# Two quantised feed-forward stages laid out with features on the partitions, two sequences a product, and the second product of a unit four steps behind its first

## The reference, cut to what matters

```python
def _L3_ffn_ref(x, qweights, scales, biases, lora_a, lora_b, ln_gamma, ln_beta):
    def _dequant(q, scale):                       # groups of 16 share a scale
        return (q.astype(jnp.float32) / 7.5 - 1.0) * jnp.repeat(scale, 16, axis=1)
    def _qlora_linear(x, q, scale, bias, la, lb):
        base = jnp.einsum('btd,od->bto', x, _dequant(q, scale)) + bias
        return base + jnp.einsum('btr,or->bto', jnp.einsum('btd,rd->btr', x, la), lb)
    def _layernorm(x, g, b):
        mu = jnp.mean(x, axis=-1, keepdims=True)
        var = jnp.mean(jnp.square(x - mu), axis=-1, keepdims=True)
        return (x - mu) * jax.lax.rsqrt(var + 1e-5) * g + b
    h = x
    for blk in range(3):
        y = _qlora_linear(h, ... 2 * blk ...)
        y = jax.nn.gelu(_layernorm(y, ln_gamma[blk], ln_beta[blk]), approximate=False)
        h = _qlora_linear(y, ... 2 * blk + 1 ...) + h
    return h
...
x = x + 0.5 * _L3_ffn_ref(_layernorm(x), ...)     # stage f3a
x = x + _L3_attn_ref(_layernorm(x), ...)          # stage at3
x = x + 0.5 * _L3_ffn_ref(_layernorm(x), ...)     # stage f3b
```

## Time and profile before

| | us |
|---|---|
| median of 3 runs | 3105.43 (3095.72 to 3110.03) |
| the profiled execution: its own time | 3106.51 |
| its span | 3104.8 |
| stage f3a, first to last instruction | 101.6 |
| stage at3 | 410.0 |
| stage f3b | 100.5 |
| mean granted TensorE clock over the span | 0.896 |

### The profile page before, as it was taken

The page is one execution under the profiler, slowest core; times in us unless marked ns, Lnnn a source line. Parts: engine busy times, 40 slices in busy tenths (PEclk is TensorE's granted clock), DMA queues, the critical chain, the costliest instruction groups (busy, mean ns, idle before and its releaser), DMA issues. The chain is left out here.

```text
span 3104.8 us, 39498 instructions
## 1 busy us (share of the span) xinstructions
PE 2575.9 (83%) x11320; PEld 1549.7 (50%) x11320; DVE 2025.0 (65%) x4275; ACT 1696.5 (55%) x3585; POOL 1243.8 (40%) x1144
## 2 busy tenths in 40 slices
PE   7999785688888888888677998688699967988975
PEld 5667532354444444444333443456444444777764
DVE  7888655699999999999644443466344364545445
ACT  4555322788888888888422443577444323555532
POOL 1000102688888888888500000322000052444444
PEclk9999898798989989989898999799899966888866
DMA  2000131333333434333332111000111100000000
GB/s 99 1 1 0 58 83 28 131 142 136 151 140 139 145 136 150 140 136 148 143 82 82 55 60 50 1 1 0 55 55 55 63 15 0 1 0 0 0 1 14
DMA packets 35669, 209.60 MB, mean 68 GB/s; under 512 B 4032, under 2 KB 5184, under 8 KB 14016
## 3 DMA queue, kind: packets, MB, share of 16 engines
q1 hardware_dynamic: 35520, 207.89, 18.8%
HBM read 205.25 MB, written 2.62 MB: 67 GB/s over the span
## 5 line engine op out<-in xcount | busy, mean ns | idle before, releaser
L1382 PE MATMUL banks<-mam_state_c,identity 128*128 128x512 f32 x1024 | 539.7, 662 | 141.8 <-POOL mam_state_c L1225 141.8
L1225 POOL TENSOR_TENSOR mam_state_c<-mam_state,weights_r 128x1024 f32<-128x1024 f32 x256 | 599.9, 2358 | 118.6 <-DVE mam_state L1173 118.5
L1173 DVE TENSOR_TENSOR_SCAN mam_state<-banks,mam_dbu 128x1024 f32<-128x1024 f32 x256 | 580.4, 2278 | 73.1 <-ACT banks L1301 72.5
L1301 ACT ACTIVATE banks<-mam_dt,mam_a_neg 128x255 f32<-128x255 f32 x1024 | 423.3, 461 | 38.3 <-DVE mam_state L1173 36.7
L1382 PEld LDWEIGHTS banks<-mam_state_c,identity 128*128 128x128 f32 x1024 | 200.1, 208 | 399.1 <-issue 199.6
L1151 DVE TENSOR_TENSOR mam_dbu<-banks,weights_r 128x1024 f32<-128x1024 f32 x224 | 267.1, 1204 | 10.4 <-ACT banks L1309 10.4
L2224 POOL TENSOR_TENSOR at_attention<-at_relu 128x512 f32<-128x512 f32 x128 | 130.9, 1040 | 172.9 <-ACT at_relu L2277 88.3
L424 ACT ACTIVATE at_probs<-banks,at_nmax 128x256 f32<-128x256 f32 x256 | 117.7, 472 | 138.4 <-DVE at_nmax L365 134.9
L2402 PEld LDWEIGHTS banks<-at_v,at_attention 128*128 128x128 f32 x1024 | 153.2, 223 | 41.0 <-issue 34.8
L862 DVE TENSOR_TENSOR m2b_hidden<-m2b_gelu,m2b_comb_spread 128x512 f32<-128x512 f32 x128 | 85.9, 690 | 129.2 <-ACT m2b_gelu L889 119.6
L862 DVE TENSOR_TENSOR m2a_hidden<-m2a_gelu,m2a_comb_spread 128x512 f32<-128x512 f32 x128 | 86.0, 690 | 128.9 <-ACT m2a_gelu L889 118.5
(11 more groups left out here) (483 smaller groups left out, 5304.6 us busy)
## 6 DMA issues: line engine op xcount, KB each, us to landing
weights_r<-mam_bc_rows SPq DMA_DIRECT2D x128, 1024.0 KB, 4.7
m2a_comb_spread<-m2a_comb_rows SPq DMA_DIRECT2D x16, 1024.0 KB, 7.6
m2b_comb_spread<-m2b_comb_rows SPq DMA_DIRECT2D x16, 1024.0 KB, 7.6
m1a_comb_spread<-m1a_comb_rows SPq DMA_DIRECT2D x16, 512.0 KB, 8.1
m1b_comb_spread<-m1b_comb_rows SPq DMA_DIRECT2D x16, 512.0 KB, 8.5
weights_r<-in_mb SPq DMA_DIRECT2D x1, 4332.0 KB, 12.8
weights_r<-in_m SPq DMA_DIRECT2D x1, 4200.0 KB, 13.1
weights_r<-in_a SPq DMA_DIRECT2D x1, 2632.0 KB, 12.1
```

What stands on the lines that cost most here:

```text
L1173: dve.tensor_tensor_scan(flat2(h[:, i % 4, :, :, :]), decay(i), flat2(dbu[:, i % 4, :, :, :]), 0.0, ALU.mult, ALU.add).then_inc(h_ready, 1)
L1225: pool.tensor_tensor(hc[:, j % 4, :, :, :], h[:, j % 4, :, :, :], c_rows(j), ALU.mult).then_inc(hc_ready, 1)
L1301: i = act.activation(decay(j)[:, o + 1:o + S], dt[:, q, c, 1:S], ACT.Exp, scale=aneg[:, l, k:k + 1])
L1382: k = pe.matmul(y_bank(q)[:, :], K.ident[:, :], flat(hc[:, j % 4, n, :, :]), start=(j == 0 and n == 0), stop=(j == NP - 1 and n == 1))
```

## The change

In both stages the activations are kept with features on the partitions, 512 tokens (a pair of sequences) wide. The weights become the stationary operand, so one product handles a pair. A unit is one block for one pair; there are 3 x 4 = 12 of them (n = 4 * block + pair), and the hardware loop is gone. The norm inside a block is rebuilt: the first weights of each block and their bias have their mean over the outputs taken off once, so that y comes out with mean zero; ACT makes y and its square (L2029, L2026), PE sums the squares over the features with four products against one column of ones (L2080), DVE turns the sum into variance plus eps (L1975), POOL takes the power -1/2 of 128x4 numbers (L2002), PE spreads the result over all partitions with four products against the identity (L2071), and DVE multiplies (L1968). The bias of the second product goes into the add of h (L1961). Transposes are left only at the entry and the exit of a stage (L2046, L2103).

The engines walk through steps m = 0 to 16. PE's list in step m holds the second product of unit m-4, the spread of unit m-2, the sum of squares of unit m-1 and the first product of unit m. The first product of unit m >= 4 needs the h that DVE makes out of the second product of unit m-4, the same pair one block earlier.

The weights are built in f3a alone and kept for f3b (K.f3_w, K.f3_b). The stage has 24 semaphores instead of 17. The packed array f3 holds 6 columns of biases instead of 768.

```diff
-    "f3": dict(scale=768, bias=768, la=768, lb=768, gam=3, bet=3),
+    "f3": dict(scale=768, bcol=6, la=768, lb=768, gam=3, bet=3),
...
-    NB, U = 3, 4
+    NB, NP = 3, B // 2
+    N = NB * NP
...
+        w = K.f3_w
+        bcol = K.f3_b
...
+        y_bank = lambda m: K.ps[m % 3]
+        r_bank = lambda m: K.ps[3 + m % 2]
+        z_bank = lambda m: K.ps[5 + m % 2]
+        t_bank = lambda p: (r_bank, z_bank)[p // 2](p)
+        b1 = lambda m: bcol[:, 2 * (m // NP):2 * (m // NP) + 1]
+        b2 = lambda m: bcol[:, 2 * (m // NP) + 1:2 * (m // NP) + 2]
+        v_cols = lambda m: K.ps[7][:, (m % 2) * 8:(m % 2) * 8 + TP]
...
+                norm_sums(0)
+                if first:
+                    dve.wait_ge(K.loaded["f3"], 16)
+                    dve.wait_ge(K.loaded_q, 16)
+                    link = chain(dve, dve_s)
+                    link(dve.tensor_scalar(w[:, :], K.qw[:, :], 7.5, 1.0 / 7.5, ALU.subtract, ALU.mult))
+                    link(dve.tensor_tensor(w[:, :], w[:, :], f("scale"), ALU.mult))
+                norm_apply_pair(0)
+                if first:
+                    dve.wait_ge(lora_ps, 1)
+                    dve.tensor_tensor(w[:, 0:512], w[:, 0:512], K.ps[0][:, :], ALU.add)
+                    link(dve.tensor_tensor(w[:, 512:768], w[:, 512:768], K.ps[1][:, 0:256], ALU.add))
+                    firsts = w[:, :].rearrange("p (b a o) -> p b a o", b=NB, a=2)[:, :, 0, :]
+                    link(dve.tensor_reduce(wmean[:, :], firsts, AX_X, ALU.add))
+                    link(dve.tensor_scalar(wmean[:, :], wmean[:, :], 1.0 / P, None, ALU.mult))
+                    dve.tensor_tensor(firsts, firsts, wmean[:, :].unsqueeze(2).broadcast_to([P, NB, P]), ALU.subtract)
+                    dve.wait_ge(bias_ps, 1)
+                    cols = bcol[:, :].rearrange("p (b a) -> p b a", a=2)
+                    dve.tensor_copy(cols[:, :, 1], f("bcol").rearrange("p (b a) -> p b a", a=2)[:, :, 1])
+                    dve.scalar_tensor_tensor(cols[:, :, 0], K.ps[2][:, 0:6].rearrange("p (b a) -> p b a", a=2)[:, :, 0],
+                                             -1.0 / P, f("bcol").rearrange("p (b a) -> p b a", a=2)[:, :, 0],
+                                             ALU.mult, ALU.add).then_inc(w_ready, 1)
+                    dve.wait_ge(w_ready, 1)
+                norm_sums(1)
+                norm_apply_pair(1)
+                for m in range(N + 5):
+                    n = m - 4
+                    if 0 <= n < N:
+                        dve.wait_ge(z_ps, n + 1)
+                        h = ht[:, n % NP, :]
+                        dve.scalar_tensor_tensor(h, z_bank(n)[:, :], b2(n), h, ALU.add, ALU.add).then_inc(h_ready, 1)
+                    n = m - 2
+                    if 0 <= n < N:
+                        dve.wait_ge(r_ps, n + 1)
+                        dve.wait_ge(y_ready, n + 1)
+                        if n >= 2:
+                            dve.wait_ge(gt_ready, n - 1)
+                        dve.tensor_tensor(yn[:, n % 2, :], yc[:, n % 3, :], r_bank(n)[:, :],
+                                          ALU.mult).then_inc(yn_ready, 1)
+                    n = m - 1
+                    if 0 <= n < N:
+                        dve.wait_ge(var_ps, n + 1)
+                        if n >= 2:
+                            dve.wait_ge(ys_ready, n - 1)
+                        dve.tensor_scalar(var[:, n % 2, :], v_cols(n), 1.0 / P, EPS, ALU.mult,
+                                          ALU.add).then_inc(var_ready, 1)
+                    if m + 2 < NP:
+                        norm_sums(m + 2)
+                        norm_apply_pair(m + 2)
+                    p = m - 5 - (NB - 1) * NP
+                    if 0 <= p < NP:
+                        dve.wait_ge(o_ps, p + 1)
+                        x = K.x[:, p * WP:(p + 1) * WP]
+                        dve.scalar_tensor_tensor(x, y_bank(m)[:, :], 0.5, x, ALU.mult, ALU.add).then_inc(added, 1)
...
+                norm_root(0)
+                norm_root(1)
+                for n in range(N):
+                    if n + 2 < NP:
+                        norm_root(n + 2)
+                    pool.wait_ge(var_ready, n + 1)
+                    if n >= 2:
+                        pool.wait_ge(r_ps, n - 1)
+                    pool.tensor_tensor(ys[:, n % 2, :], var[:, n % 2, :], K.neg_half[:, 0:TP],
+                                       ALU.pow).then_inc(ys_ready, 1)
...
+                transposed_input(0)
+                if first:
+                    act.wait_ge(w_ready, 1)
+                for m in range(N + 2):
+                    n = m - 2
+                    if 0 <= n < N:
+                        act.wait_ge(yn_ready, n + 1)
+                        if n >= 2:
+                            act.wait_ge(z_ps, n - 1)
+                        act.activation(gt[:, n % 2, :], yn[:, n % 2, :], ACT.Gelu, bias=f("bet")[:, n // NP:n // NP + 1],
+                                       scale=f("gam")[:, n // NP:n // NP + 1]).then_inc(gt_ready, 1)
+                    if m < N:
+                        act.wait_ge(y_ps, m + 1)
+                        if m >= 2:
+                            act.wait_ge(var_ps, m - 1)
+                        act.activation(sq[:, m % 2, :], y_bank(m)[:, :], ACT.Square, bias=b1(m)).then_inc(sq_ready, 1)
+                        if m >= 3:
+                            act.wait_ge(yn_ready, m - 2)
+                        act.activation(yc[:, m % 3, :], y_bank(m)[:, :], ACT.Identity, bias=b1(m)).then_inc(y_ready, 1)
+                    if m + 1 < NP:
+                        transposed_input(m + 1)
...
+                transposed_input(0)
+                if first:
+                    pe.wait_ge(w_ready, 1)
+                for m in range(N + 5):
+                    n = m - 4
+                    if 0 <= n < N:
+                        pe.wait_ge(gt_ready, n + 1)
+                        if n < 2:
+                            pe.wait_ge(ht_ready, n + 3)
+                        else:
+                            pe.wait_ge(h_ready, n - 1)
+                        c = 2 * (n // NP) + 1
+                        pe.matmul(z_bank(n)[:, :], w[:, c * P:(c + 1) * P], gt[:, n % 2, :],
+                                  start=True, stop=True).then_inc(z_ps, 1)
+                    n = m - 2
+                    if 0 <= n < N:
+                        pe.wait_ge(ys_ready, n + 1)
+                        if n < 2:
+                            pe.wait_ge(ht_ready, n + 1)
+                        else:
+                            pe.wait_ge(yn_ready, n - 1)
+                        for j in range(TP):
+                            k = pe.matmul(r_bank(n)[:, j * P:(j + 1) * P], ys[:, n % 2, j:j + 1].broadcast_to([P, P]),
+                                          K.ident[:, :], start=True, stop=True)
+                        k.then_inc(r_ps, 1)
+                    n = m - 1
+                    if 0 <= n < N:
+                        pe.wait_ge(sq_ready, n + 1)
+                        if n >= 1:
+                            pe.wait_ge(var_ready, n)
+                        for j in range(TP):
+                            k = pe.matmul(v_cols(n)[:, j:j + 1], sq[:, n % 2, j * P:(j + 1) * P], K.ones[:, 0:1],
+                                          start=True, stop=True)
+                        k.then_inc(var_ps, 1)
+                    if m < N:
+                        p = m % NP
+                        if m >= 3:
+                            pe.wait_ge(y_ready, m - 2)
+                        if m < NP:
+                            pe.wait_ge(ht_ready, m + 1)
+                        else:
+                            pe.wait_ge(h_ready, m - NP + 1)
+                        c = 2 * (m // NP)
+                        pe.matmul(y_bank(m)[:, :], w[:, c * P:(c + 1) * P], ht[:, p, :],
+                                  start=True, stop=True).then_inc(y_ps, 1)
+                        if m + 1 < NP:
+                            transposed_input(m + 1)
+                    p = m - 5 - (NB - 1) * NP
+                    if 0 <= p < NP:
+                        pe.wait_ge(h_ready, (NB - 1) * NP + p + 1)
+                        pe.wait_ge(y_ready, min(N, m - 2))
+                        if p >= 3:
+                            pe.wait_ge(added, p - 2)
+                        for j in range(TP):
+                            k = pe.transpose(y_bank(m)[:, j * P:(j + 1) * P], ht[:, p, j * P:(j + 1) * P], K.ident[:, :])
+                        k.then_inc(o_ps, 1)
...
+        K.f3_w = K.sb("f3_weights", [P, 6 * P])
+        K.f3_b = K.sb("f3_bias", [P, 6])
```

More of the change, by code:

```diff
@@ L1891, in stage_quantised_ffn @@
+        f = lambda n: field(K, "f3", n)
+        first = tag == "f3a"
+        y_bank = lambda m: K.ps[m % 3]
[5 more added lines that the diff above has]
+        v_cols = lambda m: K.ps[7][:, (m % 2) * 8:(m % 2) * 8 + TP]
         with nc.Block() as block:
@@ new lines, in norm_sums, with norm_apply_pair @@
+                def norm_sums(p):
```

(29 more changed lines are left out.)

168 lines of the change are left out of this document (27 added, 141 removed).

## The result

The changed kernel took 3012.66 us (median of 4 runs, 3005.74 to 3027.46) beside 3105.4; the ratio is 0.971 (95% interval 0.967 to 0.976). Five more runs of it had a median of 3019.70 beside 3104.07, ratio 0.973 (0.970 to 0.975). The direction and the source of the gain were as forecast. The profiled execution was the slowest of the four (3027.46 us).

The account below looks back on a forecast made before the run. Bound by a chain crossing the engines phase by phase, with PE's clock low. f3b 63.5 plus f3a 66.2 us instead of 202.1 gives -72.4; semaphores +0.9 and waits +1.5 leave -70: 3035.5 us, range 3021 to 3066.

Parts of the forecast that it names:

- Step: Middle of both stages: PE's four items take 3.47 us unhindered, the root adds 0 to 0.25; 3.60 taken.
- Entry: Stage start: DVE's four norm rounds, then step 3 and half of step 4 at low clock, +4; f3b 24.3 us.
- Weights in f3a: f3a's entry: adds, reduce, subtract and tiny operations make 2.7 us; two earlier operations hide in the first root's wait.
- Exit: End of each stage, after the first product of unit 11: a chain of 10.4 us.
- Unpriced waits, +1.5: Both stages: free banks, first uses, GELU's table load; 0 to 5 us over 17 steps twice, 1.5 taken.
- Semaphores, +0.9: After each stage: seven more semaphores to clear, 0.066 us each, +0.9.
- The other stages: Everything outside f3a and f3b, at3 between them included, was taken as left alone.
- The favourable end: Whole kernel 3025 with step 3.47, clock 1.00 at entry and no waits; below 3025 got 0.03.
- The swing: Middle steps: half run at 6.7 us as PE's clock swings, 25 us in all, 3060; chance 0.18.
- the low level: Both stages at low clock throughout: step 6.7, 25 us more a stage, 3090 in all; chance 0.07.
- The serial chain: In-order lists make units follow one another: step 9.0 us, 3138 in all, slower; chance 0.04.
- That the entry on DVE bounds a part of the stage: Stage entry: DVE binds it, so only the 8 middle steps gain; already in the sum, 24 us of 63.

Follow-up runs that it names:

- the split run: Both large products split into four of 128 columns each, against the changed kernel: f3b 58.70, f3a 62.23 us, step 3.57 us.
- the run with all norms first: Changed kernel with sums earlier, idle products (one in f3a, three in f3b), all four norms and roots ahead of the first unit: f3b 55.30, f3a 60.26 us.
- the run with idle products: Changed kernel with unread identity products ahead of the first transposes, one in f3a, four in f3b: f3b 58.03, f3a 61.56 us.
- half of the second product: Changed kernel with every second product over 256 of 512 columns: step 3.28 us; f3b gained 0.8 us, f3a 2.3.
- the repeat: The changed kernel again, no edit, against the kernel before: ratio 0.973 (0.970 to 0.975), f3a 61.57, f3b 58.03 us.
- the power twice: Changed kernel with POOL taking every unit's power twice: step 4.26 us, f3b 70.28, f3a 72.01, whole 3031.69 us (one run).
- the two runs that leave work out: Changed kernel with half of every second product, or half of every spread, left out: steps of 3.28 and 3.06 us.
- the rebuilt f3b: Changed kernel with f3b building weights, their mean and biases again, as f3a does: f3b 61.58, f3a 63.40 us.
- half of the spread: Changed kernel with two of the four column blocks of every spread left out: step 3.06 us.

## Why the prediction was right in kind and low in size

- **Bound before, source of the gain.** Right. With the units in series nothing of the gain is left, and the split run shows that the width is worth nearly nothing.
- **Step.** 3.47 by the list, 3.60 taken, 3.50 measured; 0.8 us a stage too much. The parts 0.86, 0.94, 0.81, 0.86 came out as 0.86, 0.89, 0.81, 0.94. From the end of the sum to the spread's weight load the root takes 3008.45 to 3009.93, 1.48 us (hop 0.17, power 1.01) against 1.60 to 1.97 forecast: no product waits in front of the spread, but it is the tightest feed, as said. That the power could stretch beside DVE wasn't tested by the step: DVE is idle all through it (1.67 us ahead of 3010.45). "One of DVE's SBUF operations" is too broad as well: in the run with all norms first, a power beside the application of a norm and bn_stats of 128x128 still took 1.03 us.
- **Entry: the step that failed.** "I count these 2.6 us and half of step 4 at the low level, +4". Without it the sum had 20.3 for f3b; 19.86 is measured. PE had not "mostly stood still": from the first product on it was busy nearly throughout, and the level rose 14.9 us after the start, ahead of the spread (17.1 us) from which PE goes on without a wait. The low products are there (2.07 us each), but beside DVE's rounds; the run with idle products removed some of them and gained 0.00, and with the level at 1.00 from 8.8 us on (half of the second product) y3 came no earlier. It was close: PE's sum of unit 1 ends where the third first product starts (2977.14), and DVE, just then ready for it, makes the variance behind that power; a rise 5.5 us later cost 1.83 us in f3a. In f3a the forecast was 27.0 and 23.35 is measured. These two entries are 8.1 of the 10.1 us by which the stages were over-forecast.
- **Weights in f3a.** Forecast 2.7 us, measured 3.5. The adds, the reduce and the small ones took 2.6, as forecast. The two operations that were to hide in the wait for the first root did stand in it, but the root took longer beside them: POOL's scaling and power took 0.44 and 1.72 us instead of 0.23 and 1.03, and DVE's first application came 0.97 us later than in f3b.
- **Exit.** 10.4 forecast; from the end of step 11 (3009.39) to 3019.57, 10.18.
- **Unpriced waits, +1.5.** None seen in the middle; the table load of GELU (1.28 us in f3b) was over before its input came. **Semaphores, +0.9.** From the last add to at3's first bn_stats 3.0 us instead of 2.8: +0.2 for f3a, and 0.8 less behind f3b.
- **The other stages: a second step that failed.** I had taken them as fixed ("all else is left alone"). With the terms above put right (10.1 for the stages, 1.5 for the waits, 1.4 for the seams) the forecast is 3022.5, still just inside the range. The repeat (3019.70) lies 2.8 us below that and the first median (3012.66) 9.8. at3 was 3.4 us shorter in the trace of the repeat. Of the three faster runs behind the first median there is no trace, so where their 9.8 us lie stays open.
- **The favourable end.** By its own terms it is 3023.9 and not 3025 (4 us for each entry, 16 x 0.13 and 1.5 less than 3035.5). It gives 119.6 us for both stages, and 119.63 was measured. That is partly luck: f3b came out 0.4 below it and f3a 0.4 above. I had given what lies below 3025 a chance of 0.03.
- **Rivals.** The swing and the low level did not come in the two traces of the changed kernel: 1.00 from the end of the entry on. The swing isn't far off, though: with the power twice, and in f3b of the two runs that leave work out, the level fell back to 0.50 for three to ten us around y3. In f3b it had each time risen early (8.8 to 9.0 us), as the changed kernel's own f3b might in another execution; why it falls back stays open. The Trainium skill's rule on cycling through banks (TensorE: Matmul & The Clock Gate, A second HAM failure mode: psum-queue depth-cycling) speaks of PE idling for moments between groups. Here PE goes through all eight banks in turn without a pause, at 1.00, so these traces neither bear the rule out nor refute it. The serial chain is real, and at the low level costs 11.5 us a step (from 3080.20 to the next first product, 3091.66) instead of my 9.0; the order of the lists avoids it. That the entry on DVE bounds a part of the stage is borne out: a better order there, with idle products, gave 5.2 us.

## What to carry to other kernels

In these stages a low clock cost only where PE was on the path: find first which engine sets a stretch, and add the surcharge only from where PE takes over. When the other engine gets faster, that point moves forward, and the low level begins to cost. Order the units so that each engine's list has other units' work between the ends of every hop; the same instructions in series took 2.5 times as long. Price a change of a few us by the windows of the stages it touches, not by totals, when an unchanged stage moves by 17 us with the granted clock, and compare in these windows when the level rose.

## What the hardware showed that I had not expected

- at3, in which no instruction is changed, took from 397.5 to 414.2 us, at a mean granted clock from 0.86 to 0.80. The stages ahead of f3a, unchanged too, took from 2474.0 to 2484.7 us.
- Four idle products at the start of f3a instead of one: the level rose after 7.1 us instead of 17.3, which was worth 1.2 us net of their own cost (one trace each).
- The level in f3b's entry rose 14.8 to 14.9 us after the start in the two traces of the changed kernel, and after 8.8 to 9.0 us in four others, in three of which nothing edited runs before that point. The early rise was no gift: in those three (with the power twice, half of the second product, half of the spread) it fell back to 0.50 later on.
- POOL's power of 128x4 is 1.01 us in all middle steps, the low end of the earlier trace rows, with DVE idle beside it. Beside DVE's operations on the 768 columns of the weights it is 1.72 us in f3a and 1.71 in the rebuilt f3b, where no transfer runs.
